# Roots as one power on GpSimd, side stages moved to other steps, and the first layer's score matmuls issued as pairs of row tiles

## What is computed

```python
x = x + retention(layernorm(x))     # 16 heads of 8: q, k with rotation, scores * decay,
                                    # times v, norm over each head, gain and bias, @ Wo
y = layernorm(x)
h = rms(y, n1_w)
q, k = rms(heads(h @ wq.T), qn_w), rms(heads(h @ wk.T), kn_w)
attn = softmax(where(causal, q @ k.T / sqrt(8), -inf))
y = y + (attn @ v) @ wo.T           # first 32 channels of the addend set to 0
xf = rms(y, n2_w)
moe = sum_e weight_e(xf) * expert_e(xf)     # 4 experts, top 2 of a softmax router
out = x + y + moe                   # first 32 channels of moe set to 0
```

## Time and profile before

| what | value |
|---|---|
| runs, median | 1179.03 us |
| the profiled execution's own time | 1180.29 us |
| its span, first to last instruction | 1178.1 us |
| TensorE matmuls busy | 945.5 us (80%), 6192 |
| VectorE busy | 602.3 us (51%), 1483 |
| ScalarE busy | 499.6 us (42%), 1008 |
| GpSimd busy | 314.5 us (27%), 538 |
| mean granted TensorE clock | 0.764 |

### The profile page before, as it was taken

The page is one execution under the profiler, slowest core; times in us unless marked ns, Lnnn a source line. Parts: engine busy times, 40 slices in busy tenths (PEclk is TensorE's granted clock), DMA queues, the critical chain, the costliest instruction groups (busy, mean ns, idle before and its releaser), DMA issues.

```text
span 1178.1 us, 16413 instructions
## 1 busy us (share of the span) xinstructions
PE 945.5 (80%) x6192; PEld 570.6 (48%) x6192; DVE 602.3 (51%) x1483; ACT 499.6 (42%) x1008; POOL 314.5 (27%) x538
## 2 busy tenths in 40 slices
PE   2845768878798888988799888988888888988857
PEld 1625535534545455554556455554555453544434
DVE  2544565565753566465663566455653574245021
ACT  1314215245445444444445445454445343524524
POOL 4203104213412232133412232133412220311311
PEclk9576657676789776986788776986789767857959
DMA  4000000000000000000000000000000000000000
GB/s 138 1 9 1 1 9 2 1 1 10 1 1 1 19 1 1 2 10 10 1 1 2 19 1 1 1 11 1 1 1 2 10 1 0 11 1 1 10 1 10
DMA packets 13726, 9.05 MB, mean 8 GB/s; under 512 B 2128, under 2 KB 13136, under 8 KB 13648
## 3 DMA queue, kind: packets, MB, share of 16 engines
q1 hardware_dynamic: 13648, 8.00, 2.3%
HBM read 5.64 MB, written 2.10 MB: 7 GB/s over the span
## 4 chain that ended last, share of the span: by engine, by line
PE 64%; DVE 25%; ACT 5%; issue 4%; POOL 1%; DMA 0%; SPq 0%; POOLq 0%; ACTq 0%; DVEq 0%
PE side L456 13%; PE side L343 9%; PE outs L394 7%; DVE mneg L852 7%; PE side L444 6%; PE scores L374 6%; PE maxima L356 5%; PE side L492 4%; PE side L414 4%; PE maxima L359 4%; PE outs L432 3%; PE side L439 3%; ACT p L637 2%; DVE hB L993 2%; DVE p L862 2%
## 5 line engine op out<-in xcount | busy, mean ns | idle before, releaser
L852 DVE TENSOR_REDUCE mneg<-maxima 128x2 f32<-128x256 f32 (+3 forms) x256 | 211.2, 825 | 321.3 <-PE maxima L359 319.6
L637 ACT ACTIVATE p<-scores 128x1024 f32<-128x1024 f32 (+3 forms) x256 | 180.1, 704 | 188.7 <-PE scores L374 187.5
L1079 POOL TENSOR_SCALAR_AFFINE_SELECT p<-p 128x256 f32<-128x256 f32 x256 | 106.9, 417 | 526.9 <-ACT p L637 526.8
L356 PE MATMUL maxima<-ks,qs 24*128 24x384 f32 (+3 forms) x512 | 110.8, 429 | 102.0 <-DVE mneg L852 101.7
L374 PE MATMUL scores<-qs,ks 25*128 25x256 f32 (+3 forms) x512 | 129.0, 501 | 20.5 <-ACT p L637 18.2
L356 PEld LDWEIGHTS maxima<-ks,qs 24*128 24x128 f32 x512 | 61.5, 237 | 131.5 <-DVE mneg L852 128.5
L394 PE MATMUL outs<-p,v2x 128*32 128x512 f32 (+3 forms) x1024 | 115.2, 587 | 1.0 <-POOL p L1079 1.0
L374 PEld LDWEIGHTS scores<-qs,ks 25*128 25x128 f32 x512 | 57.1, 219 | 100.0 <-issue 60.6
L359 PE MATMUL maxima<-negb,idb 128*128 128x128 bf16 x512 | 85.2, 258 | 0.0
L1087 POOL TENSOR_SCALAR_AFFINE_SELECT p<-p 128x512 f32<-128x512 f32 x64 | 41.0, 641 | 165.3 <-ACT p L646 165.3
L414 PE MATMUL side<-qs,ks 24*128 24x128 f32 x512 | 58.9, 334 | 23.7 <-DVE p L862 20.6
(11 more groups left out here) (169 smaller groups left out, 1528.0 us busy)
## 6 DMA issues: line engine op xcount, KB each, us to landing
x_in<-x_dram SPq DMA_DIRECT2D x8, 256.0 KB, 2.9
qs<-mT SPq DMA_DIRECT2D x128, 2.0 KB
out_dram<-yout SPq DMA_DIRECT2D x8, 256.0 KB, 2.3
sb_t_cos<-t_cos_dram SPq DMA_DIRECT2D x1, 512.0 KB, 4.8
sb_t_sin<-t_sin_dram SPq DMA_DIRECT2D x1, 512.0 KB, 5.0
sb_w_l<-w_l_dram SPq DMA_DIRECT2D x2, 256.0 KB
sb_w_qkv<-w_qkv_dram SPq DMA_DIRECT2D x2, 192.0 KB, 3.6
sb_w_u<-w_u_dram SPq DMA_DIRECT2D x3, 128.0 KB
```

Of the source, the lines that this page charges most:

```text
L356: nc.tensor.matmul(mb[:, i, 0:n + 128], qs[rows, b % 2, g, n:n + 128], ks[rows, b % 2, g, 0:n + 128], start=True, stop=False, skip_group_c ...
L637: A_(p2[kt][:, 2 * hp:2 * hp + 2, :], eb[:, :, 0:n], ACT.Exp, scale=float(D) ** -0.5).then_inc(exp_done, 1)
L852: V.tensor_reduce(mneg[:, g, 2 * hp:2 * hp + 2, qt], mb[:, :, 0:128 * (qt + 1)], AX.X, ALU.max, negate=True)\
L1079: Q.affine_select(out=diag, in_=diag, compare_op=ALU.is_ge, fill=0.0, base=0, pattern=[[0, 2], [1, 128]], channel_multiplier=-1).then_inc( ...
```

## The change

`rsqrt` goes. VectorE writes the variance and counts `var_ready`; GpSimd raises it to the power -0.5 in one instruction against a constant column; VectorE waits for `root_ready` a step or two later. Nearly every side stage of `before`, `lead` and `tail` gets another step, on all engines and in `SIDE_UNITS`, and in steps 28 and 30 `lead` now comes ahead of `tail`. The first layer's scores are issued as pairs of row tiles (heads 0, 1 and heads 2, 3), group by group in turn, where one tile's four groups came behind one another.

```diff
-            scratch[name] = (sb("rv_" + name, [128, n]), sb("ri_" + name, [128, n], i32), sb("ry_" + name, [128, n]),
-                             sb("rt_" + name, [128, n]))
+            scratch[name] = (sb("rv_" + name, [128, n]), sb("ry_" + name, [128, n]))
+        mhalf = sb("mhalf", [128, 1])
...
-                for j in range(J):
-                    dst = side(f"SC{t}{j}", b)
-                    rows = slice(SW * j, SW * j + SHIFT)
+                for pair in ((0, 1), (2, 3)):
+                    dst = [side(f"SC{t}{j}", b) for j in pair]
                     for g in range(G):
-                        last = nc.tensor.matmul(dst[:, 128 * g:128 * g + 128], ks1[rows, g, at], qs1[rows, g, at],
-                                                start=True, stop=True)
-                    last.then_inc(side_filled, 1)
+                        for j in pair:
+                            rows = slice(SW * j, SW * j + SHIFT)
+                            last = nc.tensor.matmul(dst[j % 2][:, 128 * g:128 * g + 128], ks1[rows, g, at], qs1[rows, g, at],
+                                                    start=True, stop=True)
+                            if g == G - 1:
+                                last.then_inc(side_filled, 1)
...
             def before(b, s):
-                rv, _, ry, _ = scratch["norm1"]
-                if s == 2:
+                rv, ry = scratch["norm1"]
+                if s == 3:
...
-                    step(V.tensor_scalar(rv[:], red[:], 1.0 / D, EPS_LN, ALU.mult, ALU.add))
-                if s == 3:
-                    rsqrt("norm1")
-                if s == 4:
+                    V.tensor_scalar(rv[:], red[:], 1.0 / D, EPS_LN, ALU.mult, ALU.add).then_inc(var_ready["norm1"], 1)
+                if s == 5:
+                    dve.wait_ge(root_ready["norm1"], count(root_ready["norm1"], b, 1))
...
+            def root(b, name):
+                rv, ry = scratch[name]
+                pool.wait_ge(var_ready[name], count(var_ready[name], b, 1))
+                Q.tensor_tensor(ry[:], rv[:], mhalf[:].broadcast_to([128, rv.shape[1]]), ALU.pow).then_inc(root_ready[name], 1)
```

More of the change, by code:

```diff
@@ L47 @@
     NF + 1: [(1, "N1"), (-1, "MT3")],
[L48 to L51, removed]
+    NF + 2: [(-2, "DN1")],
+    NF + 4: [(2, "XN"), (-2, "DN2")],
+    NF + 6: [(-2, "DN3")],
+    NF + 7: [(1, "ON")],
+    NF + 8: [(1, "WO1")],
     NF + 9: [(0, "MT0")],
-    NF + 10: [(1, "H")],
-    NF + 11: [(1, "Q20"), (1, "Q21")],
-    NF + 12: [(1, "Q22"), (1, "Q23")],
+    NF + 13: [(1, "H")],
+    NF + 14: [(1, "Q20"), (1, "Q21")],
+    NF + 15: [(1, "Q22"), (1, "Q23")],
     NF + 17: [(0, "MT1")],
[L57 to L62, removed]
-    NF + 25: [(0, "MT2")],
-    NF + 26: [(2, f"S10{g}") for g in range(G)],
-    NF + 27: [(-1, "XF")],
-    NF + 28: [(2, f"S11{g}") for g in range(G)] + [(-1, "GATE")],
+    NF + 20: [(-1, "N20"), (-1, "N21"), (2, "Q10"), (2, "Q11")],
+    NF + 21: [(2, "Q12"), (2, "Q13")],
+    NF + 22: [(1, f"S21{g}") for g in range(G)] + [(-1, "AO")],
+    NF + 23: [(1, f"S20{g}") for g in range(G)],
+    NF + 24: [(-1, "WO2")],
+    NF + 25: [(0, "MT2")],
+    NF + 26: [(2, "QT")],
+    NF + 27: [(2, "ST")],
+    NF + 28: [(2, f"S10{g}") for g in range(G)],
+    NF + 29: [(-1, "XF")],
+    NF + 30: [(2, f"S11{g}") for g in range(G)] + [(-1, "GATE")],
 }
@@ L285, in build @@
         dve_step = sem("dve_step")
+        var_ready = {name: counted("var_ready_" + name) for name in scratch}
+        root_ready = {name: counted("root_ready_" + name) for name in scratch}
         def count(s, b, n):
@@ L789, in _ @@
                 for place in range(NF):
+                    if place == 0 and on(it - 2):
+                        tail(it - 2, G * GK)
                     if place in (0, 3, 5) and on(it + 1):
@@ L807, in _ @@
                         maxima_transposed(it + MT_AT[s][0], MT_AT[s][1])
+                    if s in (28, 30) and on(it + 2):
+                        lead(it + 2, s)
                     if on(it - 1):
                         tail(it - 1, s)
-                    if on(it + 2):
+                    if s not in (28, 30) and on(it + 2):
                         lead(it + 2, s)
@@ L944, in before @@
                     i.then_inc(z_ready, 1)
[L945 to L946 removed]
+                rv, ry = scratch["norm2"]
+                if s == 17:
                     for m in range(2):
@@ L974, in lead @@
             def lead(b, s):
-                rv, _, ry, _ = scratch["lead"]
+                rv, ry = scratch["lead"]
                 if s == 3 - NF:
@@ L1099, in down @@
                 Q.tensor_tensor(yout[:, t, M0:C], yout[:, t, M0:C], weighted[:, t, 0, :], ALU.add).then_inc(out_ready, 1)
+            def root(b, name):
+                rv, ry = scratch[name]
+                pool.wait_ge(var_ready[name], count(var_ready[name], b, 1))
+                Q.tensor_tensor(ry[:], rv[:], mhalf[:].broadcast_to([128, rv.shape[1]]), ALU.pow).then_inc(root_ready[name], 1)
             def before(b, s):
-                if s in (12, 13):
-                    m = s - 12
+                if s == 3:
+                    root(b, "norm1")
+                if s == 10:
+                    root(b, "pre")
+                if s == 17:
+                    root(b, "norm2")
+                if s in (15, 16):
+                    m = s - 15
                     pool.wait_ge(raw2_ready, count(raw2_ready, b, 2 * m + 2))
@@ L1130, in lead @@
             def lead(b, s):
-                if s == 21:
+                if s == 4 - NF:
+                    root(b, "lead")
+                if s == 23:
                     pool.wait_ge(raw1_ready, count(raw1_ready, b, NT))
@@ L1148, in tail @@
             def tail(b, s):
-                if s == 25:
+                if s == 26:
+                    root(b, "tail")
+                if s == 27:
                     pool.wait_ge(y_ready, count(y_ready, b, 1))
@@ L1177, in _ @@
                         masked(it + 1, {0: 0, 1: 1, 3: 2, 5: 3}[place])
+                    if on(it + 2):
+                        lead(it + 2, place - NF)
                 for s in range(G * GK):
```

163 lines of the change are left out of this document (80 added, 83 removed).

## The result

The changed kernel takes **1319.63 us** (median of 4 runs, 1319.24 to 1319.95) against 1179.58 us of the kernel before beside it: a ratio of 1.118 (95% interval 1.116 to 1.120). It is 140 us slower.

The account below looks back on a forecast made before the run. A step lasts the longest of TensorE's work, the row-maximum loop and VectorE's work between reductions. 2.5 us idle plus 5.0 clock a turn, times 7, is 52; fill 9, tail 2: 63 us, so 1116 us, range 1068 to 1165.

Parts of the forecast that it names:

- rival 3: Slower than before: the 128-column power costs over about 9 us, stalling VectorE at step 19; 1206 us at 12 us; 6%.
- The power's price: GpSimd's power at 128 columns: 0.47 us from below, 5.2 from above; taken near the low end, so no stall.
- norm1's cover: Time the new table gives norm1's root on GpSimd before VectorE wants it: 4.7 us.
- The place of the stall: With a dear power, VectorE waits for norm2's root at step 19, with L852 and all maxima behind it.
- The schedule without the price: The whole change with powers that cause no stall: 63 us gained, TensorE's idle time 15.4 against 17.94 us a turn.
- The largest gain, steps 14-16: TensorE's idle time there falls from 4.92 to 0.5 us, with projections Q2 on 14 and 15 and the chain gone.
- The new empty steps: Steps without side matmuls on TensorE: 3.0 us idle in steps 10-13, 3.5 in steps 17-20.
- The clock: TensorE's low clock level holds 47 us a turn instead of 59, giving 5.0 us a turn.
- rival 4: The clock recovers much more, low for 30 us a turn: 114 us gained, 1066 us; 13%.
- The fill and the tail: Fill up to 134.8 us: four chains (11 us) go, powers take 2 back, gaining 9; last tail chain gives 2.
- The pairs: First layer's scores as pairs of row tiles: costed at nothing, third tile 1.5 us later, fourth at the same time.
- Rival 5: Old order ran score tiles one at a time, so pairs save 0.5 us eight times a batch, 32 us: 1084 us; 5%.

Follow-up runs that it names:

- run 1: The changed kernel with a GpSimd product in the place of each power (roots left out, output not the reference's): 1099.1 us, ratio 0.926.
- and old order (6): The changed kernel with products for the powers (roots left out) and the scores back to one tile after the other: 1070.0 us, ratio 0.902.
- experiment 5: The kernel before with only the first layer's score matmuls issued as pairs of row tiles: 1202.3 us, ratio 1.015.
- experiment 8: The changed kernel with its powers kept and only the scores' order put back to one tile after the other: 1335.1 us, ratio 1.131.

## Why the prediction was wrong

The forecast was 1116 us and 93% for faster. The kernel did what **rival 3** describes, which had 6%.

- **The power's price** is the step that failed: "I take a price nearer to the low end (one instruction of a kind this engine has rows for), up to twice it, and so no stall". The prediction took 0.47 us at 128 columns, with 5.2 us as the upper bound; measured are 20.73 us, 44 times and 4 times these. At 64 columns it is 10.53 (bound 3.7), at 8 1.64, at 4 1.02. The bounds came from rows of products and masks, and no row of this kernel had a power in it. That the chain's own length bounds the price was an assumption that no row bore out; how GpSimd computes a power no run shows. Even rival 3, which saw "nothing in the trace excludes it", was priced at 12 us.
- **The rest of that reasoning holds: what VectorE's own work does not cover stands on its queue.** With the measured prices in the prediction's own terms, the stalls are (20.73 - 2.1) + (10.53 - 4.7) + (1.64 - 0.9) + (1.02 - 0.7) = 25.5 us a batch, 204 us in all, and 1116 + 204 = 1320 us, against 1319.6. That it meets the measured time to 1 us is luck: the base was 17 us too high (1099 for 1116), and norm1's cover too large by 19 us in eight batches. It was "4.7"; in turn 4 VectorE waited 8.22 us of 10.54, so 2.3 us were covered. VectorE came to the wait 3.8 us behind the variance, and for 1.5 of them the root stood behind the sums of the down projection on GpSimd's queue (733.20 and 733.55 against 731.89 in the rows above); that queue was missing in the sum. norm2's cover was put at 2.1 and is 1.9 (20.73 less 18.80).
- **The place of the stall.** Forecast: step 19, with the reduction and all maxima behind it. VectorE does stand there, but TensorE's long wait is at step 20 for the side buffer of N20. Same cause, other link.
- **The schedule without the price** gained 84 us (run 1) where 63 were forecast. By stretch, TensorE's idle time in a turn (length less busy, as in the earlier trace rows):

| steps | 0-2 | 3-5 | 6-9 | 10-13 | 14-16 | 17-20 | 21-24 | 25-26 | 27-30 | 31, places | sum |
|---|---|---|---|---|---|---|---|---|---|---|---|
| before | 0.46 | 0.81 | 2.04 | 0 | 4.92 | 1.57 | 1.72 | 2.56 | 1.14 | 2.72 | 17.9 |
| forecast | 0 | 1.0 | 1.3 | 3.0 | 0.5 | 3.5 | 1.3 | 0.1 | 0.9 | 3.8 | 15.4 |
| changed | 0.04 | 6.08 | 1.37 | 1.60 | 0.85 | 20.06 | 0.19 | 0.88 | 0.16 | 4.82 | 36.1 |
| product (1) | 0.04 | 0.53 | 1.01 | 1.31 | 0.85 | 0.82 | 0.18 | 0.88 | 1.58 | 4.83 | 12.0 |
| and old order (6) | 0.04 | 0.54 | 1.01 | 1.49 | 0.85 | 0.94 | 0.19 | 0.89 | 1.59 | 2.27 | 9.8 |

 The largest gain, steps 14-16, was right (4.1 us for 4.4). The new empty steps were feared too much: 1.31 for 3.0 in steps 10-13 and 0.82 for 3.5 in steps 17-20. "Most of their time comes back as empty steps" was wrong: 5.9 us a turn are gained in run 1, not 2.5.
- **The clock**, "the softest term", was put at 5.0 us a turn. Run 1 shows 7.7 (busy 115.15 to 107.44 at 0.78 to 0.86), between the forecast and rival 4; the changed kernel 4.4, although its clock is 0.77: 20.1 of its 36.1 idle us lie in a stretch at 0.55, and the 32.0 us of work of the last stretch run at 0.91. That this is all of it, no run shows. The seven turns from the first to the eighth's start gave 89 us in run 1 (872.07 to 783.32) for the 52 forecast.
- **The fill and the tail**: 9 and 2 us forecast; in run 1 3.8 us (134.8 to 131.1), and the end from the last turn on is 11 us longer, at a clock of 0.70 where before had 0.76. In the changed kernel the fill is 30 us longer, with the first batch's powers (33.9 us, where the chains took 11) on its only path.
- **The pairs**, "I cost at nothing", cost 1.5% in the old schedule and 2.4% in the new one with products. The mechanism stood in the text (the third tile 1.5 us later); that step went wrong in giving it no price. In four comparisons of the same schedule (old, changed, with products, with chains) the pairs add 13.0, 16.0, 15.0 and 17.2 us of idle time ahead of the score products; the time follows in two, is unclear with chains, and goes the other way in the changed kernel, by the clock. TensorE's idle time at the places was forecast at 3.8 for another cause, VectorE's logits; the pairs make up 2.6 of the 4.8 measured.
- **Rival 5**, the program-order rule of the Trainium skill, "TensorE: Matmul & The Clock Gate", section "Part 3: Packing small matmuls — row/col tiling", falls: 12 products in 0.68 us in the old order, 8 in 0.66 us in pairs, and pairs that cost time (experiment 5) where the rival had 32 us of gain.

## What to carry to other kernels

Before a function is moved to another engine, measure that one instruction there at the shapes in use; here a row of another operation on the same engine bounded nothing, and a chain of many cheap instructions may be the shorter. An instruction's price per column decides where it may stand: narrow powers (1.0 to 1.6 us) were worth it here, wide ones were not. With few buffers in rotation, count what an order asks for at once and when it gives it back: two of three at once made TensorE wait 13 to 17 us longer here, and the products themselves gained nothing.

## What the runs showed of the hardware

- GpSimd's power takes about 0.40 us and 0.159 us a column (0.56 us at 1, 2.91 at 16, 10.5 at 64, 20.7 at 128), whatever the partitions (32 or 128) and the exponent (-0.5 or 1.0), both tried at 64 columns. The Trainium skill, "GPSIMD Engine Reference", section "4.1 Engine selection", puts two-input elementwise work there at about twice VectorE's time; by that and VectorE's 0.38 us for one at 128 columns, an estimate of 0.8 us. The product at 128 columns took 0.40 us (experiment 1), half of that estimate; the power took 20.73, 52 times the product.
- TensorE's clock can outweigh the idle time that caused an edit to be made: 2.1 us less of idle and 8.9 us more of busy time in a turn of the same matmuls (experiment 8). An edit that saved some 2 us of idle time a turn came out with the other sign.
